# Token scores in four quarters of 32 rows: four maxima, or two score matmuls, side by side

## What is computed

```python
enc, ca = ctx[:, :2044], ctx[:, 2044:]            # 2044 text rows, 4 tokens, of 384
hs = mha(x @ Wq, enc @ Wk, enc @ Wv)
ca_q1 = einsum('btc,th->bch', ca, Wq_ca)          # 384 queries of 640, of rank 4
ca_hs1 = mha(ca_q1[:, indices], x, x)             # 1024 gathered from the 384
ca_hs2 = mha(ca_hs1 @ Wq, ca @ Wk_ca, ca @ Wv_ca)
out = (hs + ca_hs2) @ Wout + b_out + x
```

## Time and profile before

| | |
|---|---|
| time, median of 3 runs | 1240.54 us (1239.85 to 1242.08) |
| the profiled execution | 1241.22 us, its span 1239.4 us |
| TensorE busy | 1217.6 us, 98% of the span |
| TensorE weight loads | 959.3 us, 77% |
| VectorE busy | 830.7 us, 67% |
| ScalarE busy | 678.4 us, 55% |
| GpSimdE busy | 206.5 us, 17% |
| mean granted clock of TensorE | 0.997 of full speed |

### The profile page before, as it was taken

How to read it: one execution, slowest core, us unless ns; L and a number is a source line. 1 busy time by engine, 2 the same in 40 slices (tenths; PEclk the granted TensorE clock), 3 DMA queues, 4 the chain that set the end, 5 groups by cost and what they waited for, 6 DMA issues and landing times.

```text
span 1239.4 us, 14524 instructions
## 1 busy us (share of the span) xinstructions
PE 1217.6 (98%) x5644; PEld 959.3 (77%) x5644; DVE 830.7 (67%) x1167; ACT 678.4 (55%) x773; POOL 206.5 (17%) x114
## 2 busy tenths in 40 slices
PE   7999999998999999999999999999999999999998
PEld 6889988896766667777777777777777777776898
DVE  6348825591234368888878878878888888887452
ACT  5232324222444456777677677677677777767310
POOL 1100000001000011222222322221221221222133
PEclk9999999999999999999999999999999999999999
DMA  8995899896650063254254254344345436422254
GB/s 303 275 320 184 227 279 242 278 276 146 190 156 1 1 160 105 87 150 99 73 149 107 70 145 107 92 122 108 108 115 123 102 96 150 116 79 64 68 209 149
DMA packets 96575, 180.68 MB, mean 146 GB/s; under 512 B 17289, under 2 KB 50057, under 8 KB 92378
## 3 DMA queue, kind: packets, MB, share of 16 engines
q1 hardware_dynamic: 88938, 157.33, 47.3%
q0 software_dynamic: 2816, 11.80, 3.1%
q10 hardware_dynamic: 4752, 10.62, 2.5%
HBM read 116.32 MB, written 63.24 MB: 145 GB/s over the span
## 4 chain that ended last, share of the span: by engine, by line
PE 94%; DMA 3%; DVE 1%; ACT 1%; issue 1%; SPq 0%; ACTq 0%
PE at_ps L1226 28%; PE at_ps L1207 19%; PE bank L646 18%; PE at_ps L206 9%; PE acc_t_ps L1003 6%; PE at_ps L1399 6%; PE bank L623 2%; PE s_ps L970 2%; DMA q_lo_d<-out_lo 1%; PE bank L593 1%; PE f_ps L943 1%; DMA v_lo_d<-v_t 1%; DMA wqT<-in_wqT 1%; PE acc_t_ps L981 1%; DVE prob_lo L1085 1%; PE f_ps L932 1%
## 5 line engine op out<-in xcount | busy, mean ns | idle before, releaser
L214 DVE TENSOR_REDUCE mpart<-at_ps 128x1 f32<-128x512 f32 x480 | 326.3, 686 | 109.6 <-PE at_ps L206 107.9
L1148 ACT ACTIVATE prob_hi<-at_ps 128x1024 fp32r<-128x1024 f32 (+1 forms) x256 | 263.1, 1028 | 196.9 <-PE at_ps L1207 196.9
L1226 PE MATMUL at_ps<-prob_hi,v 128*81 128x512 f32 (+1 forms) x1024 | 318.8, 396 | 0.2 <-issue 0.2
L1085 DVE TENSOR_TENSOR prob_lo<-probs,prob_hi 128x1024 fp32r<-128x1024 f32 (+1 forms) x211 | 270.7, 1283 | 20.4 <-ACT probs L1153 20.3
L1153 ACT ACTIVATE probs<-at_ps 128x1024 f32<-128x1024 f32 (+1 forms) x256 | 261.2, 1020 | 0.0
L1226 PEld LDWEIGHTS at_ps<-prob_hi,v 128*81 128x81 f32 (+1 forms) x1024 | 153.6, 151 | 59.3 <-issue 6.1
L1085 POOL TENSOR_TENSOR prob_lo<-probs,prob_hi 128x1024 fp32r<-128x1024 f32 x45 | 108.1, 2402 | 519.3 <-ACT probs L1153 519.3
L206 PE MATMUL at_ps<-a 128*128 128x512 f32 x480 | 193.9, 404 | 0.0
L206 PEld LDWEIGHTS at_ps<-a 128*128 128x128 f32 x480 | 153.7, 320 | 31.8 <-DVE mpart L214 0.8
L1207 PE MATMUL at_ps<-a 128*128 128x512 f32 (+1 forms) x512 | 161.5, 396 | 1.2 <-ACT probs L1153 0.6
L1226 PE MATMUL at_ps<-prob_lo,v 128*81 128x512 f32 (+1 forms) x512 | 160.0, 394 | 2.3 <-DVE prob_lo L1085 2.3
(11 more groups left out here) (142 smaller groups left out, 1426.5 us busy)
## 6 DMA issues: line engine op xcount, KB each, us to landing
v_hi_d<-v_t SPq DMA_DIRECT2D x16, 648.0 KB, 8.9
v_lo_d<-v_t SPq DMA_DIRECT2D x16, 648.0 KB, 11.7
v<-v_hi_d SPq DMA_DIRECT2D x16, 648.0 KB, 4.8
v<-v_lo_d SPq DMA_DIRECT2D x16, 648.0 KB, 5.9
k_hi_d<-out_hi SPq DMA_DIRECT2D x40, 256.0 KB, 5.5
k_lo_d<-out_lo SPq DMA_DIRECT2D x40, 256.0 KB, 6.4
a<-k_hi_d SPq DMA_DIRECT2D x16, 640.0 KB, 7.7
b<-k_hi_d SPq DMA_DIRECT2D x16, 640.0 KB, 11.3
```

Of the source, the lines that this page charges most:

```text
L214: dve.tensor_reduce(self.mpart[:, g % 2, qt, c:c + 1], mx_ps[k % 2][:, 0:w], AX, ALU.max).then_inc(self.mx_done, 1)
L1085: eng.tensor_tensor(pl[n % PB][0:r, :], prob[n % PF][0:r, :], ph[n % PB][0:r, :].bitcast(F32), ALU.subtract).then_inc(sem, 1)
L1148: act.activation(ph[n % PB][0:r, :], s_ps[n % 2][0:r, :], ACT.Exp, scale=SCALE).then_inc(ph_done, 1)
L1226: mm = pe.matmul(o_ps[:, u * CH:(u + 1) * CH], a[0:r, t, :], y[n % PB][0:r, u * CH:(u + 1) * CH], start=t == 0 and m == 0, stop=t == KT - ...
```

## The change

The token operands get another layout. `token_row` puts head `h` in quarter `h % 4` of 32 rows, at row 0 or 16 of it by `h // 4`; its 16 rows are high, high by low and low by high of its 4 tokens, a row of ones against the negative maximum, and three of nothing. The two heads of a quarter have separate column blocks in `ca`, `[P, B*2*CD]`, which now holds both batches. `marks` has the signs by which ScalarE (L535) and VectorE make high and low parts in all 128 rows at once. `ca2` and `u2` are copies turned by two quarters (`turn`, two DMAs each), so that the two score matmuls of a step use different quarters.

- A maximum is a matmul over 32 rows. They come four in a row, one in each quarter: 12 groups a batch, 5 of them in the `q` jobs of chunk 1, then 4 and 3 in chunks 2 and 3 (`GROUPS_AT`).
- A score pair is two matmuls over 32 rows each in two different quarters.
- `shift_tokens` issues two DMAs a head. Those of batch 0 stand in the projection's SyncE queue.
- `wqT` lies over `x_lo` and is loaded in batch 1's chunk 2. The second making of batch 0's operand in the token stage is gone.
- `early_split` stands in tiles 6 to 15 of the last head, and GpSimdE waits for its end before it adds the bias.
- The last output tile is made, added and stored in two halves.

```diff
-CA_PARTS = 4
+GROUPS_AT = {("q", 1): (0, 1, 2, 3, 4), ("k", 2): (1, 3), ("v", 2): (2, 5), ("k", 3): (0, 2, 4)}
+def token_row(h):
+    return 32 * (h % 4) + 16 * (h // 4)
+def token_columns(h):
+    return slice(h // 4 * CD, (h // 4 + 1) * CD)
+def quarter(h, turned=False):
+    q = (h + 2 * turned) % 4
+    return slice(32 * q, 32 * (q + 1))
...
-        jobs, maxima = [], [("m", 0, (hc, u)) for hc in range(NH * KC) for u in range(2)]
+        jobs = []
+        maxima = [(top, kc, u) for u in range(2) for top in range(NH // 4) for kc in range(KC)]
+        def with_maxima(some, c):
+            for i, job in enumerate(some):
+                jobs.append(job)
+                if i in GROUPS_AT.get((job[0], c), ()):
+                    top, kc, u = maxima.pop(0)
+                    jobs.extend(("m", u, (4 * top + r, kc, u)) for r in range(4))
...
+        def turn(sp, to, a, columns, sem):
+            for half in range(2):
+                rows, from_rows = slice(64 * half, 64 * half + 64), slice(64 - 64 * half, P - 64 * half)
+                sp.dma_start(to[rows, columns].bitcast(F32), a[from_rows, columns].bitcast(F32)).then_inc(sem, 16)
...
-                    if b == B - 1 and n == last_m + 2:
-                        sp.wait_ge(top_done, 2 * B)
-                        shift_tokens(sp, kept, ca, b, range(0, NH, 2))
+                    if n == last_m + 2:
+                        sp.wait_ge(top_done, 2 * (b + 1))
+                        sp.wait_ge(kept["ca2_in"], 32)
+                        shift_tokens(sp, kept, b, range(0, NH, 1 if b < B - 1 else 2))
+                    if (kind, c, m) == ("k", NQ, 0):
+                        sp.wait_ge(done, b * NJ + last["u", NQ - 1] + 1 + 8)
+                        turn(sp, u2, u_all, slice(b * SQ, (b + 1) * SQ), kept["u2_in"][b])
+                        if b == 0:
+                            sp.wait_ge(ca_lo, 1)
+                            turn(sp, ca2, ca, slice(0, B * 2 * CD), kept["ca2_in"])
...
+                        sp.dma_start(kept["wqT"][:], d["wqT"].rearrange("(m p) n -> p m n", p=P)
+                                     ).then_inc(kept["wqT_in"], 16)
...
-                        sp.dma_start(kept["ca_f"][0:K3, 0:NH * CD], d["caBD"][0]).then_inc(kept["ca0_in"], 16)
...
+            def split_ca():
+                act.wait_ge(ca_in, 16)
+                act.activation(ca[:], ca_f[:, 0:B * 2 * CD], ACT.Identity, scale=marks[:, 3:4]).then_inc(ca_hi, 1)
...
-                        if (hc, u) == (0, 0):
-                            pe.wait_ge(ca_lo, b + 2)
-                            pe.wait_ge(done, b * NJ + last["u", NQ - 1] + 1 + 8)
-                        at = hc // KC * CD + hc % KC
-                        pe.matmul(bank[:], ca[0:K3, at:at + (P - 1) * KC + 1:KC],
-                                  u_all[0:K3, bass.ds(b * SQ + u * CH, CH)], start=True, stop=True
+                        if (h, kc) == (0, 0):
+                            pe.wait_ge(ca_lo, 1)
+                            pe.wait_ge(done, b * NJ + last["u", u] + 1 + 8)
+                        at = b * 2 * CD + token_columns(h).start + kc
+                        pe.matmul(bank[:], ca[quarter(h), at:at + (P - 1) * KC + 1:KC],
+                                  u_all[quarter(h), bass.ds(b * SQ + u * CH, CH)], start=True, stop=True
...
-                    mm = pe.matmul(s_ps[k % 2][:, t, 0:CD],
-                                   kept["u"][0:K3 + 1, b * SQ + st * P:b * SQ + (st + 1) * P],
-                                   ca[b][0:K3 + 1, h * CD:(h + 1) * CD], start=True, stop=True)
+                    st, rows = 2 * j + t, quarter(h, t == 1)
+                    mm = pe.matmul(s_ps[k % 2][:, t, 0:CD], u[t][rows, b * SQ + st * P:b * SQ + (st + 1) * P],
+                                   ca[t][rows, col:col + CD], start=True, stop=True)
...
-            if t == 1:
+            first = KT - 2 * MC
+            if t == first:
                 dve.wait_ge(at.s_full, (G - 1) * KT)
...
             pool.wait_ge(bias_in, 16)
+            pool.wait_ge(lo[1], MC)
...
-                for m in range(MC):
-                    for k, (a, y) in enumerate(products((high[i], whole[i]), wout)):
-                        for u in range(2):
...
+                for us in ((0, 1),) if n < LAST else ((0,), (1,)):
+                    for m in range(MC):
+                        for k, (a, y) in enumerate(products((high[i], whole[i]), wout)):
+                            for u in us:
```

More of the change, by code:

```diff
@@ L83, in place_before, with place_row @@
             return t
+    def place_row(self, *tensors):
+        with ExitStack() as row:
+            return [row.enter_context(self.nc.sbuf_tensor(*t)) for t in tensors]
     def psum(self, name, shape, dt=F32):
@@ L320, in project @@
         last = {(kind, c): n for n, (kind, c, _) in enumerate(jobs)}
-        last_m = last["m", 0]
+        last_m = last["m", 1]
         def read_ctx(c):
@@ L488, in scalar @@
                     elif kind == "u":
-                        dst = u_all[0:K3, bass.ds(b * SQ + c * CH, CH)]
-                        act.activation(dst, banks[n % 8][0:K3, :], ACT.Copy).then_inc(hi_done, 1)
+                        if b == 0 and c == 0:
+                            act.wait_ge(marks_in, 16)
+                        dst = u_all[:, bass.ds(b * SQ + c * CH, CH)]
+                        act.activation(dst, banks[n % 8][:], ACT.Identity, bias=marks[:, 2:3], scale=marks[:, 0:1]
+                                       ).then_inc(hi_done, 1)
                     else:
@@ L661, in project, with shift_tokens @@
         return Stage(sync, gpsimd, scalar, vector, tensor), written, evicted
-def shift_tokens(eng, kept, ca, b, some):
+def shift_tokens(eng, kept, b, some):
     for h in some:
-        row = ca[K3:K3 + 1, h * CD:(h + 1) * CD].rearrange("o (p c) -> o p c", c=KC)
-        eng.dma_start(row.bitcast(F32), kept["ntop"][:, b, h * KC:(h + 1) * KC].bitcast(F32)
-                      ).then_inc(kept["ntop_in"][b][h], 16)
+        for i, ca in enumerate((kept["ca"], kept["ca2"])):
+            r = quarter(h, i == 1).start + 16 * (h // 4) + 3 * NT
+            at = b * 2 * CD + token_columns(h).start
+            row = ca[r:r + 1, at:at + CD].rearrange("o (p c) -> o p c", c=KC)
+            eng.dma_start(row.bitcast(F32), kept["ntop"][:, b, h * KC:(h + 1) * KC].bitcast(F32)
+                          ).then_inc(kept["ntop_in"][b][h], 16)
 def tokens(nc, outer, kept, at, written, evicted, d, scratch):
@@ L676, in tokens @@
         s = Scope(nc, stack, outer.sems)
-        wqT = s.sb("wqT", [P, MC, HID])
+        wqT = kept["wqT"]
         wout = wqT
@@ L751, in sync @@
             sp.dma_start(kept["wk2"][:], d["wk2_frame"]).then_inc(wk2_in, 16)
-            sp.dma_start(wqT[:], rows(d["wqT"])).then_inc(wqT_in, 16)
-            shift_tokens(sp, kept, ca[0], 0, range(NH))
             sp.wait_ge(wk2_full, 1)
@@ L1360, in scalar @@
                     act.activation(high[i], whole[i].bitcast(F32), ACT.Copy).then_inc(hi[i], MC)
+            act.wait_ge(done, NT_OUT + 1)
+            act.dma_start(out[LAST * P:(LAST + 1) * P, HALF:HID], o_t[LAST % NO][:, HALF:HID]
+                          ).then_inc(o_out[LAST % NO], 16)
             for i in range(NO):
-                act.wait_ge(o_out[i], 16 * len(range(i, NT_OUT, NO)))
+                act.wait_ge(o_out[i], 16 * (len(range(i, NT_OUT, NO)) + (i == LAST % NO)))
         def vector(dve):
@@ L1425, in program @@
             "small_in": s.sem("small_in"),
-            "ca0_in": s.sem("ca0_in"),
+            "u2_in": [s.sem(f"u2_in{b}") for b in range(B)],
+            "ca2_in": s.sem("ca2_in"),
             "xn1_in": [s.sem(f"xn1_in{j}") for j in range(ST // 2)],
```

175 lines of the change are left out of this document (86 added, 89 removed).

## The result

The changed kernel took 1247.48 us (median of 13 runs, 1243.11 to 1251.42). The kernel before, on the same chip, took 1240.63 us (13 runs, 1238.77 to 1242.08). The ratio is 1.0053, with an interval of 1.0037 to 1.0068. The prediction was 1230.7 us and faster; the time is inside its range of 1212 to 1250, the sign is wrong. That the range holds the time is owed to the lower half of rival B, which it took in, and not to the forecast's sum. Rival B's sign came, but as the experiments show, only a part of it came by B's mechanism.

The account below looks back on a forecast made before the run. TensorE, busy 98% of the span, was taken as the bound, so only its path counted. Terms -5.1 - 1.9 - 2.0 - 0.5 + 1.1 - 8.4 - 3.8 + 8.8 + 2.0 = -9.8 took 1240.5 to 1230.7 us, range 1212 to 1250.

Parts of the forecast that it names:

- rival B: Each change between full rows and quarters empties TensorE: 1256 us at 0.2 us a change, 1270 at 0.28; chance 0.22.
- wait for `wqT`: Token stage: TensorE's 5.09 us wait for this load goes, as the load comes earlier; -5.1 us.
- half clock behind it: Behind the `wqT` wait, 80 matmuls take 6.2 us at full clock instead of 8.09; -1.9 us.
- last head: TensorE's waits of 1.28 and 1.01 us for low parts shrink; -2.0 us, bounds -2.3 and 0.
- `ca` earlier: Projection: `ca` is needed one chunk earlier and TensorE waits for it once; +1.1 us.
- maxima with their 48 changes: Projection: 24 groups of four take 0.58 us instead of 0.93, -8.4 us; their changes of rows cost +2.4.
- score pairs with their 128 changes: Token stage: 64 pairs take 0.30 us instead of 0.36, -3.8 us; their changes of rows cost +6.4.
- the DMA term: Stores and loads running past the projection delay `v_t` and the first `ntop` rows; +2.0 us, bounds 0 and 7.
- Rival C: Late stores hold up the first token steps by 7 us, and half clock adds 2: 1237 us; chance 0.10.
- s = 0.05: TensorE's price in us for each of 176 changes between full rows and quarters, +8.8 us; s could reach 0.28.
- A: Quarter matmuls run fully side by side, groups 0.23 us, pairs 0.18: 1209 us at best, 1218 at s = 0.05; chance 0.18.
- D: Quarter matmuls don't run side by side; four maxima still take 0.93 us, a pair 0.36: 1241 us; chance 0.08.

Follow-up runs that it names:

- twelfth experiment: Changed kernel with token scores over all 128 rows and unread matmuls (24 and 4) filling the wait at the token start: 1227.29 us, ratio 0.9887.
- first experiment: Changed kernel with head 0's row moves in batch 1 issued by GpSimdE ahead of the odd heads': 1233.01 us, ratio 0.9986.
- seventh experiment: Changed kernel with head 0's row moves first, and both token scores and maxima over all 128 rows: 1227.3 us, ratio 0.9895.
- third experiment: Changed kernel with head 0's row moves first and both scores of a pair in the same quarter: 1248.94 us, ratio 1.0109.
- fourth experiment: Kernel before with only the new `wqT` place and load, the later `early_split` and bias, and the halved last tile: 1228.99 us, ratio 0.9941.
- second: Changed kernel with head 0's row moves first and token scores over all 128 rows: 1221.54 us, ratio 0.9880.
- tenth experiment: Changed kernel with head 0's row moves first, two steps' scores in a row, and 5 and 4 unread matmuls in the pauses: 1220.85 us, ratio 0.9868.

## Why the prediction was wrong, point by point

| term | predicted | measured |
|---|---|---|
| wait for `wqT` | -5.1 | -5.1 |
| half clock behind it | -1.9 | -2.5 |
| last head | -2.0 | -2.4 |
| last tile | -0.5 | -0.8 |
| `ca` earlier | +1.1 | +0.5 |
| maxima with their 48 changes | -8.4 + 2.4 = -6.0 | -5.9 |
| score pairs with their 128 changes | -3.8 + 6.4 = +2.6 | +9.3 |
| start of the token stage (the DMA term) | +2.0 | +5.4 wait, +13.7 clock |
| rest of the projection | 0 | -5.2 |
| sum | -9.8 | +7.0 |

The half clock behind the wait for `wqT` is 157.1 - 5.1 - 149.5, the twelfth experiment's stretch taken from before's. The rest of the projection is the remainder of -10.7. The row of the score pairs holds both what the pairs save and what their changes cost, 158.8 - 149.5.

**The step that failed first: the DMA term.** It was right that head 0's rows would be late (0 to 3 us were named, with 7 as the bound), and wrong in two sizes. The first is the wait, 5.3 us where the term had 2.0. The backlog of transfers, to which the prediction put it down, is there: the move took 8.7 us to land, where the first of before took 2.5. What the prediction did not see is that SyncE would issue head 0's moves behind its key stores, although head 0 is needed first: in the first experiment, with the same backlog, GpSimdE's earlier issue brings the wait down to 0.50 us. The second is the clock: the text gave it "no cause to fall". That sentence was about `wqT`, but no term of the forecast held a half clock at the token start. Rival C did, with 2 us; the rows for it were those behind the wait for `wqT`, 6.8 us at half clock. After almost the same wait the stretch was 30.7 us and cost 13.7. C had the right mechanism, a late transfer and the half clock behind it, with a price seven times too small (and its own terms give 1237.7, not 1237). The earlier trace rows showed one such stretch, behind full-row work, and the text took its length for that of any.

**The second: s = 0.05.** I took it nearer to the earlier trace rows, whose changes of shape cost nothing. They are no changes of row tiling. In the token loop it is 0.16 to 0.19; around a group of maxima the trace gives 0.46 for both, 0.23 each, if the four matmuls themselves count as 0.23, which is an assumption. The emptied pipeline of the earlier trace rows, with 0.12 to 0.28, was the right neighbour. The Trainium skill ("TensorEngine Tiling (Array Packing)", Key Properties) says that changing the tiling mode drains TensorE. By that rule s stood near its upper end, and the trace agrees with 0.16 to 0.23.

**Two errors that cancelled.** In the maxima the loads were not in series (0.23 us of work for four, by the same assumption, and not 0.58), so the saving was larger than taken, and the changes dearer; -6.0 was right for wrong reasons. In the pairs the same two errors don't cancel: there are 0.18 us to save and two changes to pay, against 0.70 in a group of four. The Trainium skill ("TensorE: Matmul & The Clock Gate", Measured speedup vs the span model) gives a factor of 3.07 for four such matmuls. No rows here give that much: the four last 0.57 us from first start to last end against 1.11 in a row (seventh experiment), a factor of 1.95, and between full-row neighbours it is 0.93 / 0.69 = 1.35.

**Rival B.** Its price of 0.2 is nearly there, and so are the weights that "cannot lie ready": none is loaded ahead across a change. Whether TensorE empties in full the trace does not tell. Its time of 1256 was not met: it kept the loads in series. Without the wait, and at full clock, the kernel with all its changes of rows (174 in the trace, since the first two pairs stand in a row) takes 1230.5 us (first experiment), 4 us less than the fastest run of before on that chip (1234.3). So B alone would not have made it slower; C's mechanism had to come too. A is right inside the group, D falls by the third experiment: in one quarter a step takes 1.99 us, in two 1.82.

**What was not foreseen for the better.** The projection gained 5.2 us more than its terms. The idling of 1.19 us at 69.24, 1.4 with a second wait behind it, is gone; it is gone in the fourth experiment as well, with the places alone, whose projection is 2.1 us shorter than before's. The first 45 matmuls were done 1.0 us sooner in the profiled run, which those of the second and seventh experiments did not share. Of the other 2.8 us the seventh shows 2.6, so they have nothing to do with the quarters. Some of them lie in the pitch of the full-row matmuls: the 120 with `x_lo` as an operand follow one another every 0.236 us before, and every 0.228 in the changed kernel and 0.227 in the fourth experiment, 1.0 us in all, and the other matmuls of 512 columns gain one or two ns each, some 0.7 us. `x_lo` has another place in memory in these two kernels than before; whether that is the reason is not shown.

**The marks set in the prediction.** Group 0.91, or 0.46 for A and 1.16 for B and D: 0.81 us from the last matmul ahead to the first behind, and another 0.11 behind that. Step 1.69, 1.47 or 2.0: 1.82. No wait for `wqT`, none over 0.5 us in the last head: both held (the longest there is 0.2). Clock 1.00 throughout: wrong. Wait of 0 to 3 us at the token start: 5.28.

## What to carry to other kernels

Narrow matmuls side by side pay only by what stands between two changes of row tiling. Here a visit to the quarters costs 0.35 us in the token loop and up to 0.46 around the maxima: four matmuls of 512 columns gain 0.25, two of 384 columns lose 0.17, four of two steps break even in two quarters and gain 0.17 in four (3.29 and 3.12 us for two steps, against 3.29). So first bring the narrow work together, then tile it.

When an earlier stage is made faster, look at who issues the first thing that the next stage needs, on which queue, and what transfers are under way by then. And price a pause of TensorE with the clock behind it: 5.3 us of waiting cost 13.7 more, and matmuls that nothing reads, put in the wait, gave these back in six of ten runs.

## What the runs showed of the hardware that I had not expected

- Four matmuls in four quarters, each with weights of its own, start 3 to 4 ns apart, and all four are done in 0.57 us where one takes 0.558. Their weights are loaded only when the group starts. The 0.117 us pitch of short full-row matmuls in the earlier trace rows says nothing about them.
- Into the quarters and out again costs 0.34 to 0.36 us in the token loop, with one, two or four quarters in use. The chain of waits divides it as 0.18 to 0.20 in and 0.16 out, the starts as 0.09 ahead and 0.26 behind.
- The granted clock stayed at 1.2 GHz for 30.7 us with only 0.63 us of idling in them, and in the profiled run of the tenth experiment it fell for 20.5 us with no idle time at all. After the same wait of 5.6 us, with full-row scores, it was short in seven runs and long in three.
- Quarter scores in every step, without the long wait or with it filled, left 15 of 40 runs at full clock; full-row scores left 15 of 15.
